# Stream stage: ScalarE's queue loads the sorted expert tiles, and their products stand later in the plan

## The reference

```
q, k, v = src@Wq+bq, src@Wk+bk, src@Wv+bv          # 16 heads of 8
attn = softmax(q k^T / sqrt(8)) v @ Wo + bo
x = layer_norm(src + attn, ln1)
expert = floor(x @ router_w + router_b) mod 4       # one expert per token
ff = relu(x @ W1[expert] + b1[expert]) @ W2[expert] + b2[expert]
return layer_norm(x + ff, ln2)
```

## Time and profile before

| | |
|---|---|
| median of 3 runs | 4833.11 us (4823.82 to 4839.2) |
| profiled execution | 4847.35 us, span of its instructions 4845.5 |
| PE busy | 3972.9 us, 82% |
| DVE busy | 3183.2 us, 66% |
| ACT busy | 2805.1 us, 58% |
| POOL busy | 1147.4 us, 24% |
| granted TensorE clock, mean | 0.878 |
| load of the slots by SP | 8 times, 704 KB each, median 7.0 us to landing |

### The profile page before, as it was taken

How to read it: one execution, slowest core, us unless ns; L and a number is a source line. 1 busy time by engine, 2 the same in 40 slices (tenths; PEclk the granted TensorE clock), 3 DMA queues, 4 the chain that set the end, 5 groups by cost and what they waited for, 6 DMA issues and landing times.

```text
span 4845.5 us, 92928 instructions
## 1 busy us (share of the span) xinstructions
PE 3972.9 (82%) x37240; PEld 1659.8 (34%) x37240; DVE 3183.2 (66%) x4646; ACT 2805.1 (58%) x5448; POOL 1147.4 (24%) x1376
## 2 busy tenths in 40 slices
PE   4888867877788768873998989888999999898982
PEld 2334344343344435551223232323222222233232
DVE  4777524444443367744987868677789999787832
ACT  2677622323212245430877778677889888777771
POOL 3221011010100103332222616162212122242413
PEclk7999988798886877865999999999999999999996
DMA  2222001001100000002113222222111111314112
GB/s 79 59 59 55 14 16 23 22 2 22 23 1 1 0 8 1 1 1 63 42 32 96 64 77 65 71 70 60 41 22 48 48 35 29 91 42 110 50 52 92
DMA packets 141118, 204.34 MB, mean 42 GB/s; under 512 B 51906, under 2 KB 88770, under 8 KB 140436
## 3 DMA queue, kind: packets, MB, share of 16 engines
q1 hardware_dynamic: 123924, 137.97, 11.5%
q0 software_dynamic: 16768, 60.49, 4.3%
HBM read 123.34 MB, written 64.68 MB: 39 GB/s over the span
## 4 chain that ended last, share of the span: by engine, by line
PE 54%; DVE 21%; ACT 7%; issue 6%; POOL 6%; DMA 4%; SPq 2%; POOLq 0%; DVEq 0%; ACTq 0%
PE ps L1117 11%; DVE stream_max_pieces L1317 8%; PE ps L1090 7%; PE ps L1102 5%; PE ps L545 3%; PE ps L1887 3%; PE ps L1203 2%; PE ps L504 2%; PE ps L1211 2%; PE ps L2578 1%; PE ps L255 1%; PE ps L1964 1%; PE ps L1963 1%; PE ps L1956 1%; ACT stream_probs L1229 1%
## 5 line engine op out<-in xcount | busy, mean ns | idle before, releaser
L1317 DVE TENSOR_REDUCE stream_max_pieces<-ps 128x2 f32<-128x1024 f32 x1536 | 1795.5, 1216 | 384.2 <-PE ps L1102 376.7
L1229 ACT ACTIVATE stream_probs<-ps 128x512 f32<-128x512 f32 x3072 | 1654.4, 600 | 335.5 <-PE ps L1090 313.3
L1117 PE MATMUL ps<-stream_probs,stream_v 128*16 128x256 f32 x12288 | 989.7, 395 | 31.7 <-issue 30.3
L1102 PE MATMUL ps<-stream_k_stack,stream_q_stack 48*128 48x512 bf16 x3072 | 661.9, 396 | 107.5 <-DVE stream_max_pieces L1317 75.2
L1090 PE MATMUL ps<-stream_q_stack,stream_k_stack 51*128 51x512 bf16 x3072 | 680.7, 396 | 24.5 <-ACT stream_probs L1229 8.2
L684 DVE TENSOR_REDUCE alibi_max_pieces<-ps 128x2 f32<-128x1024 f32 (+3 forms) x384 | 355.4, 952 | 140.2 <-PE ps L529 130.8
L625 ACT ACTIVATE alibi_probs<-ps 128x512 f32<-128x512 f32 (+3 forms) x768 | 333.8, 492 | 175.6 <-PE ps L510 142.0
L1117 PEld LDWEIGHTS ps<-stream_probs,stream_v 128*16 128x16 f32 x12288 | 203.8, 94 | 672.5 <-issue 390.0
L1090 PEld LDWEIGHTS ps<-stream_q_stack,stream_k_stack 51*128 51x128 bf16 x3072 | 181.9, 93 | 675.4 <-ACT stream_probs L1229 501.4
L309 POOL CAST stream_negmax_parts<-stream_negmax_t 128x32 bf16<-128x32 f32 x96 | 20.4, 212 | 1084.5 <-DVE stream_negmax_t L1306 1071.9
L1835 PE MATMUL ps<-delta_w_delta,ident 128*128 128x512 f32 x400 | 217.5, 676 | 63.0 <-DVE delta_branch_means L2209 28.3
(11 more groups left out here) (443 smaller groups left out, 5596.6 us busy)
## 6 DMA issues: line engine op xcount, KB each, us to landing
stream_q_terms_dram<-stream_q_parts SPq DMA_DIRECT2D x72, 256.0 KB
stream_k_terms_dram<-stream_k_parts SPq DMA_DIRECT2D x72, 256.0 KB
stream_q_stack<-stream_q_terms_dram SPq DMA_DIRECT2D x96, 192.0 KB
stream_k_stack<-stream_k_terms_dram SPq DMA_DIRECT2D x96, 192.0 KB
delta_v_shifted<-delta_v_padded SPq DMA_DIRECT2D x64, 158.0 KB, 3.5
alibi_q_terms_dram<-alibi_q_parts SPq DMA_DIRECT2D x24, 256.0 KB
alibi_k_terms_dram<-alibi_k_parts SPq DMA_DIRECT2D x24, 256.0 KB
alibi_q_stack<-alibi_q_terms_dram SPq DMA_DIRECT2D x32, 192.0 KB
```

What stands on the lines that cost most here:

```text
L1102: ins = e.matmul(c.ps[:, mbank(key) + r, :], qs[R, buf, pair, qt * P:(qt + 1) * P], ks[R, buf, pair, kh * 512:kh * 512 + 512], start=True, ...
L1117: ins = e.matmul(c.ps[32 * j:32 * j + 16, 7, Q], v[:, b % 2, kt, GH * g + j, :], pr[:, (u + j // 2) % RP, j % 2, Q], start=(n == 0 and k = ...
L1229: e.activation(pr[:, u % RP, r, :], c.ps[:, ebank(key), :], ACT.Exp, scale=SCALE).then_inc(s_ed, 1)
L1317: e.tensor_reduce(mx[:, j % 2, kh, 4 * pair + qt % 4, :], c.ps[:, mbank(key):mbank(key) + 2, :], AXX, ALU.max).then_inc(s_md, 1)
```

## The change

The load of the slots (`slots`) leaves SP's list and goes to ScalarE's, with its three waits: all 128 increments of the scatters, the first clearing of the slots, and the end of the last layer norm of the moe batch before. It stands in row 68 instead of 70. The pieces behind it move back by 7 to 12 rows: xsT from 73 to 80, h from 77 to 88, w2 from 86 to 97 (the last from 119 to 131), the later weight gathers from 88 to 98, ystore from 121 to 132, gather from 126 to 138, the last stats and scale from 145 and 146 to 156 and 157. Nothing else is altered.

```diff
--- before.py
+++ after.py
@@ -895,18 +895,18 @@
         yield 36, ("rank", n)
         yield 53, ("scatter", n)
         for j in range(ET):
-            yield (37, 40, 43, 46, 63, 67)[j] if j < NWB else 88 + 8 * ((j - NWB) // 2), ("weights", n, j)
-        yield 70, ("slots", n)
+            yield (37, 40, 43, 46, 63, 67)[j] if j < NWB else 98 + 8 * ((j - NWB) // 2), ("weights", n, j)
+        yield 68, ("slots", n)
         for g in range(3):
-            yield 73 + g, ("xsT", n, g)
+            yield 80 + g, ("xsT", n, g)
         for j in range(ET):
-            yield 77 + 4 * j, ("h", n, j)
+            yield 88 + 4 * j, ("h", n, j)
         for i in range(ET // 2 + 1):
-            yield min(86 + 8 * i, 119), ("w2", n, i)
-        yield 121, ("ystore", n)
-        yield 126, ("gather", n)
-        yield 145, ("stats", n, 1)
-        yield 146, ("scale", n, 1)
+            yield min(97 + 8 * i, 131), ("w2", n, i)
+        yield 132, ("ystore", n)
+        yield 138, ("gather", n)
+        yield 156, ("stats", n, 1)
+        yield 157, ("scale", n, 1)
 
     def lay(self):
         at = {}
@@ -1238,6 +1238,12 @@
             kind, n = key[:2]
             if kind == "unit":
                 unit(n)
+                continue
+            if kind == "slots":
+                e.wait_ge(s_sc, 16 * TPB * (nth(n) + 1))
+                e.wait_ge(s_zx, 16)
+                wait(e, s_dw, (TPB + 1) * nth(n))
+                e.dma_start(xs[:, :, :], xd.rearrange("(j p) d -> p j d", p=P)).then_inc(s_xl, 16)
                 continue
             if kind == "rsqrt":
                 for i in range(2):
@@ -1579,12 +1585,7 @@
 
         for key in plan.rows:
             kind, n = key[:2]
-            if kind == "slots":
-                e.wait_ge(s_sc, 16 * TPB * (nth(n) + 1))
-                e.wait_ge(s_zx, 16)
-                wait(e, s_dw, (TPB + 1) * nth(n))
-                e.dma_start(xs[:, :, :], xd.rearrange("(j p) d -> p j d", p=P)).then_inc(s_xl, 16)
-            elif kind == "ystore":
+            if kind == "ystore":
                 e.wait_ge(s_md, M.done(("w2", n, ET // 2)))
                 wait(e, s_yg, 16 * TPB * nth(n))
                 e.dma_start(yd.rearrange("(j p) d -> p j d", p=P), xs[:, :, :]).then_inc(s_yl, 16)
```

## The result

The changed kernel takes 4783.73 us, the median of 8 runs (4763.41 to 4804.44), the kernel before beside it 4830.73: a ratio of 0.9902, 95% interval 0.9879 to 0.9924, or 47 us less. Its profiled execution took 4775.1 us (span 4773.3), 72 less than that of before. Of these 72, 29 lie ahead of the stream stage, which the change doesn't touch: the clearing of `stream_slots`, with which the stage begins, starts at 2207.2 in the trace of before and at 2178.0 in that after. So I compare stages, from this clearing to the end of the span: 2638.3 us before, 2595.3 after, **-43.0**. Differences of a few microseconds between single traces are therefore not read as effects.

A forecast was written before the change was run, and what follows sets the result against it. PE sets the stream stage's pace, its largest idleness being waits for the slots load, late through SP's turn. -84.4 + 2.7 + 12 + 2 + 4.5 = -63 us, from 4833.1 to 4770, range 4747 to 4800.

The forecast's parts named there:

- The stall: PE's wait for the slots load at the expert-tile transposes, six batches: gone with later rows and timely issue, -84.4 us.
- ScalarE's wait: ScalarE at row 68 waits for the scatters, taken to land in 5.2 us: +12 us, +2 for a falling clock.
- the control of the earlier trace: Batch 10, rows 66 to 82, without a noted wait of PE for the load: 23.93 us, the base for the stalled batches.
- ScalarE's issue: ScalarE issues the load itself, at SP's 0.38 us for each of seven batches: +2.7 us (0 to 7).
- The second scale: POOL's second scale moves to row 29, where POOL, busy for 24% of the span, has room: 0 us.
- The gather and VectorE at row 32: The later gather delays POOL's scale(n,0) by some 4.5 us; VectorE at row 32 has 9.0 us of cover: 0.
- The end: Batch 10's last products, store and gather fall past the last unit, delaying POOL's batch 11 statistics: +4.5 us (0 to 9).
- A: Rival: the wait moves to ScalarE, scatters landing in 10.8 us; gain only 20 us, 4813 us; chance 0.12.
- C: Rival: max rows come late at row 80, beside the load, 10 us in six batches; +10 us, 4843 us; chance 0.03.
- B: Rival: the issuing engine does not matter, only later rows help; 21 us of stall stay, 4780 us; chance 0.10.

The follow-up runs named there:

- 5: The changed kernel with POOL's three 128x1024 operations of the second scale cut to 128x64 in all but the last batch, nothing moved: 4844.11 us, 0.9879 of the kernel before.
- 4: The changed kernel with only POOL's second scale moved from row 157 to 186: 4842.48 us, 0.9882 of the kernel before.
- 7: The changed kernel with the second scale at row 186 and the load at 72: 4732.63 us, 0.9789 of the kernel before; with stops 4830.75 us, 0.9844.

## Why the prediction held, and which of its terms did not

The median fell by 47.0 us (forecast -63) to 4783.7 (forecast 4770, range 4747 to 4800). The sum was made for the stage; there it is -43.0.

- *The stall, -84.4.* It went entirely: no wait of PE for the load until the end. SP's turn was late, as read from the earlier trace rows.
- *ScalarE's wait, +12 and +2 of clock.* The mechanism was right, also PE's 0.5 us of cover, but the landing of 5.2 us was too short. It was 8.0, 6.3, 6.4, 5.7, 6.1 and 6.8 us; the waits are 4.0, 2.6, 6.1, 6.6, 2.4 and 3.1, in all 24.9 against 15 (each holds some 0.5 us of the issue). To compare with the control of the earlier trace rows, the control itself fell from 23.93 to 20.84 by moved work, so the six stalled stretches have fallen by 69.8 - 6 x 3.1 = 51 us beyond it, where the forecast said 68. What came back is thus 33 us (84.4 - 51), not 17: 24.9 of wait, issues included, and some 8, most likely the clock's: it was granted at 0.52 from 2545 to 2549 behind the wait of batch 0, and at 0.50 behind those of 2 and 3. The 4.0 to 10.8 of the weight gathers was the better row to size it by than the return of the max rows.
- *ScalarE's issue, +2.7.* Its rows say 0.37 to 0.39 us each: right.
- *The second scale, 0.* This is the step that failed: "POOL, busy for 24% of the span, has room there". It has room, but VectorE has none beside it. +19.0 us in rows 34 to 50, shown to be POOL's hold by 5 and given back by 4 and 7. The trace of before could have told it: its batch 10 has a cast of 2.19 us beside L1060, 2 us behind the last row.
- *The gather and VectorE at row 32, 0.* No wait of L1401 for POOL: right.
- *The end, +4.5.* +6.3, within its 0 to 9. The store took 5.1 us (4635.48 to 4640.56) instead of 4.1.
- *What was missing on the other side.* The sum so far is -51 + 19 + 6 = -26; the stage gained 43. The other 17 us are -10.7 in rows 18 to 34, +5.3 in rows 2 to 18, some -11 net from row 66 on, where the moved products lie, and -1 elsewhere. The -10.7 is not POOL's hold: in rows 18 to 34, VectorE's instructions that took over 0.1 us more than the shortest of their kind lost 4.3 us before and 13.4 after, so the hold grew there. What fell is PE's wait for the row maxima, from 15.4 to 7.3 us in these rows; which moved piece did that was not tested.

So the forecast was too good by 16 at ScalarE's wait, 19 at the scale and 2 at the end, and too poor by 17 elsewhere: 20 us in sum, -43 instead of -63. The 17 that nobody forecast are luck. With -26 in place of -43 the kernel would have stood at about 4801 (4783.7 + 17), just outside the range.

*The rivals.* A did not come: no scatter took 10.8 us. C did not come: L1090 waits for no max rows at row 80. B, "only the later rows help", at 4780, came nearer in its number, though not for its reason in this kernel: the 21 us of stall that it left to PE are there under SP (23.1), and gone under ScalarE. The issuing engine does matter to the load, but what it saves is spent again in front of the new issuer. The Trainium skill (DMA: Bandwidth & Descriptors, Issuing engines are not separate DMA queues) says that another issuer saves only the time to issue; at row 68 the result is as if it were so (0.9902 and 0.9912), at row 72 ScalarE's issue was not tested against SP, and no run here shows what SP would give with the scale moved.

## What to carry to other kernels

A DMA moved to another engine's list takes its waits with it: put it in the row where they are already over (here four rows further, 8.3 to 8.6 us behind the last scatter where it came without a wait), or the engine that computes pays what the sync engine had paid. An engine that is a quarter busy is not free: before its wide operations are moved, look at which short VectorE operations they will lie beside. And when a rearrangement moves a dozen pieces, sum the time by fixed stretches of the loop; a loss of 19 us beside a gain of 73 shows only there.

## What the runs showed of the hardware

- A VectorE cast of 8 columns that starts just behind a POOL operation takes as long as that one: 0.17 us alone, 0.32 beside 128x64, 2.35 beside 128x1024. Reductions of 1024 columns beside a 128x1024 operation kept their 1.2 us.
- A scatter of 128 rows has landed 2.25 to 2.27 us after its issue with little traffic beside it (44 to 55 GB/s), as one of two or as the last of eight; as the last of eight in the changed kernel, behind the stores of the k terms, it took 5.7 to 8.0.
- In eight traces PE, ScalarE and VectorE stood idle, mostly together, in nearly every run of eight indirect DMAs of POOL that had attention beside it: 14 to 21 idle times of ScalarE per trace, 65 to 97 us in sum, the longest 10.0, ended by something "remote". The other six traces, three of them of kernels that have the stops elsewhere, show none. Where they occur, the kernel before was 72 us slower by its medians (4902.4 to 4830.7) and the changed kernel 89. What they are, and why the changed kernel loses more, is open.
